# Delta rule: packed 32-key products sent between the stores and the scatters of the inverted blocks

## The reference

```python
def step(S, inp):
    qt, kt, vt, gt, bt = inp
    S = S * gt[..., None]
    pred = jnp.einsum('bhk,bhkv->bhv', kt, S)
    delta = (vt - pred) * bt[..., None]
    S = S + kt[..., None] * delta[:, :, None, :]
    o = jnp.einsum('bhk,bhkv->bhv', qt, S)
    return (S, o)
...
_, o = jax.lax.scan(step, S0, (tfirst(q), tfirst(k), tfirst(vf), tfirst(g), tfirst(beta)))
```

## Time and profile before

| | |
|---|---|
| median of 3 executions | 1822.89 us (1809.54 to 1831.44) |
| profiled execution, its own time | 1815.07 us |
| its span | 1813.3 us |
| TensorE, matmuls | 1519.7 us busy, 84% |
| VectorE | 1239.9 us busy, 68% |
| ScalarE | 1025.5 us busy, 57% |
| granted TensorE clock over the span | 0.881 |

### The profile page before, as it was taken

The page is one execution under the profiler, slowest core; times in us unless marked ns, Lnnn a source line. Parts: engine busy times, 40 slices in busy tenths (PEclk is TensorE's granted clock), DMA queues, the critical chain, the costliest instruction groups (busy, mean ns, idle before and its releaser), DMA issues. The chain is left out here.

```text
span 1813.3 us, 41435 instructions
## 1 busy us (share of the span) xinstructions
PE 1519.7 (84%) x14936; PEld 1014.4 (56%) x14936; DVE 1239.9 (68%) x3815; ACT 1025.5 (57%) x2716; POOL 41.2 (2%) x49
## 2 busy tenths in 40 slices
PE   6877889788797678888988888889888988878678
PEld 3534555564454245656666666666666666667435
DVE  5759989856723578777778867877866877864131
ACT  5417878876311556676666756667656656643210
POOL 0000000000000000000000000000000000000000
PEclk9888899889998689899889978989978988968599
DMA  3032000000101211111111111111210211110010
GB/s 149 25 74 69 10 10 4 2 1 1 73 0 27 68 18 44 49 46 27 51 42 31 57 50 17 55 53 22 55 48 16 60 48 18 46 24 14 1 49 23
DMA packets 118312, 67.18 MB, mean 37 GB/s; under 512 B 93648, under 2 KB 107216, under 8 KB 116960
## 3 DMA queue, kind: packets, MB, share of 16 engines
q1 hardware_dynamic: 118112, 64.54, 12.9%
HBM read 51.36 MB, written 6.98 MB: 32 GB/s over the span
## 5 line engine op out<-in xcount | busy, mean ns | idle before, releaser
L1576 DVE SCALAR_TENSOR_TENSOR arena<-arena 128x1024 f32<-128x1024 f32 x144 | 184.6, 1282 | 32.4 <-ACT arena L1151 31.0
L819 PE MATMUL bank<-xt,arena 128*128 128x512 f32 x384 | 195.3, 642 | 5.4 <-ACT arena L1143 4.0
L1654 DVE TENSOR_TENSOR arena<-arena 128x512 f32<-128x512 f32 x224 | 156.2, 697 | 14.6 <-PE bank L872 13.1
L669 PE MATMUL bank<-xt,arena 128*128 128x512 f32 x320 | 143.3, 604 | 3.8 <-DVE arena L1394 3.8
L819 PEld LDWEIGHTS bank<-xt,arena 128*128 128x128 f32 x384 | 72.7, 206 | 72.4 <-issue 70.9
L669 PEld LDWEIGHTS bank<-xt,arena 128*128 128x128 f32 x320 | 60.7, 194 | 87.2 <-issue 87.2
L688 PE MATMUL bank<-arena 128*128 128x256 f32 (+2 forms) x384 | 100.2, 409 | 6.2 <-DVE arena L1394 5.3
L1084 ACT ACTIVATE arena<-arena 128x128 f32<-128x128 f32 x256 | 99.1, 389 | 9.4 <-DVE arena L1504 9.4
L902 PE MATMUL bank<-arena 64*64 64x64 f32 x1024 | 50.4, 258 | 58.0 <-issue 55.2
L872 PEld LDWEIGHTS bank<-arena 128*32 128x32 f32 x5120 | 62.4, 120 | 65.4 <-issue 51.8
L1697 DVE SCALAR_TENSOR_TENSOR arena<-arena,bank 128x128 f32<-128x128 f32 x112 | 38.7, 345 | 87.0 <-PE bank L968 84.9
(11 more groups left out here) (170 smaller groups left out, 3516.3 us busy)
## 6 DMA issues: line engine op xcount, KB each, us to landing
arena<-d_w SPq DMA_DIRECT2D x16, 519.0 KB, 6.4
arena<-beta_scratch SPq DMA_DIRECT2D x16, 512.0 KB, 5.5
arena<-zero_scratch SPq DMA_DIRECT2D x14, 512.0 KB, 4.6
arena<-arena SPq DMA_DIRECT2D x64, 64.0 KB, 2.6
arena<-zero_scratch SPq DMA_DIRECT2D x15, 256.0 KB, 2.9
arena<-w_scratch SPq DMA_DIRECT2D x2, 1376.0 KB, 6.1
arena<-f_idx SPq DMA_DIRECT2D x2, 1072.0 KB, 11.9
w_scratch<-arena SPq DMA_DIRECT2D x2, 1072.0 KB, 4.0
```

The lines of the kernel that those rows point to most:

```text
L669: last = pe.matmul(bank[2 * w + n % 2][0:rows, :], (WU if f < 2 else WU1R)[:, w, k, m * P:m * P + rows], XT[:, k, hf * HALF:(hf + 1) * HAL ...
L819: last = pe.matmul(bank[b][:], DW[:, par, c:c + P], XT[:, k, rhs], start=(k == 0), stop=(k == KC - 1))
L1576: dve.scalar_tensor_tensor(out=CT[:, x], in0=RAW[:, x, 3 - j:3 - j + S], scalar=DW[:, par, tap:tap + 1], in1=CT[:, x], op0=ALU.mult, op1=A ...
L1654: dve.tensor_tensor(kq, kq, left, ALU.mult)
```

## The change

The four strip DMAs of a head, with the two waits ahead of them, move from a function of their own, called between `blocks` and `inverse`, into `inverse`: behind the two stores of the inverted blocks and ahead of the wait for the stores' landing. The number of DMAs, their sizes and their semaphores stay. Lines of the changed kernel behind the spot have other numbers: the stores are L545 and L546, the strips L552, the scatters L558 and L559.

```diff
--- before.py
+++ after.py
@@ -536,14 +536,6 @@
                     wait(sp, base_step, BASE_STEPS * m)
                     sp.dma_start(BL, blk_in.rearrange("b (j i) -> b j i", j=BLK)).then_inc(blocks_in, 16)
 
-                def strips(m, par):
-
-                    sp.wait_ge(strips_ready, 2 * m + 2)
-                    wait(sp, full[6], read(6, m - 2, "predict", NT - 1))
-                    for k in range(P // STRIP):
-                        ks = slice(STRIP * k, STRIP * (k + 1))
-                        sp.dma_start(MB[ks, par, :, :, ks], MBC[ks, par]).then_inc(strips_put, 16)
-
                 def inverse(m, par):
 
                     sp.wait_ge(base_step, BASE_STEPS * (m + 1))
@@ -552,6 +544,12 @@
                     wait(sp, y_put, 16 * NB * m)
                     sp.dma_start(blk_y.rearrange("b (c i) -> b c i", c=BLK), ZI).then_inc(inverse_out, 16)
                     sp.dma_start(blk_x.rearrange("b (i c) -> b i c", i=BLK), ZT).then_inc(inverse_out, 16)
+
+                    sp.wait_ge(strips_ready, 2 * m + 2)
+                    wait(sp, full[6], read(6, m - 2, "predict", NT - 1))
+                    for k in range(P // STRIP):
+                        ks = slice(STRIP * k, STRIP * (k + 1))
+                        sp.dma_start(MB[ks, par, :, :, ks], MBC[ks, par]).then_inc(strips_put, 16)
                     sp.wait_ge(inverse_out, 32 * (m + 1))
                     wait(sp, x_zero, 16 * m)
                     wait(sp, y_zero, 16 * (m - 1))
@@ -578,7 +576,6 @@
                     if m + 2 < H:
                         head(m + 2, m % 2)
                     blocks(m, m % 2)
-                    strips(m, m % 2)
                     inverse(m, m % 2)
                     if m + 2 < H:
                         gate_weights(m + 2, m % 2)
```

## The result

The changed kernel takes 1750.66 us, the median of 4 executions (1749.14 to 1755.34), against 1816.22 us of the kernel before on the same chip (1803.75 to 1831.44): a ratio of 0.9665 with a 95% interval of 0.9597 to 0.9734. Run again beside the later experiments it took 1752.17 us, a ratio of 0.9703 (0.9679 to 0.9727) to 1807.5 us. The prediction was 1749 us. The profiled execution after took 1755.34 us, the one before 1815.07. Ratios and their intervals are taken without the executions that a lower granted clock made slow, medians with them, so a ratio is not exactly the quotient of the medians beside it.

The account below looks back on a forecast made before the run. TensorE was taken to stand, with VectorE, for SyncE's DMA queue ahead of each head's first `left`. 1815.07 - 39.5 (chain) - 34 (clock) = 1741.6 us against the profiled execution, 1749 against the median; range 1730 to 1793 us.

Parts of the forecast that it names:

- What bounds the kernel: Ahead of each head's first `left`, TensorE (57.9 us in all) and VectorE (84.9 us) stand still for SyncE's queue.
- The stores go first: In SyncE's queue, stores issue inside the wait for level 4, so the first scatter goes 2.65 us earlier, 2.0 in head 0.
- How much of 2.65 us counts: At the first `left`, the earlier scatter counts only where TensorE pauses that long: 39.5 us over sixteen heads.
- TensorE's clock: Behind the first `left`, shorter pauses remove 87 us of low clock time, at 0.39 us each: 34 us.
- if low time moves into the levels: Sign of being wrong: low clock time turns up at the matmuls of the levels; no size given.
- the rival in which the clock gives nothing: In the delta rule, falls of the clock only move to the levels' small matmuls; 39.5 us remain, 1783 us; chance 0.25.
- The sum: Whole kernel: 1815.07 - 39.5 - 34 = 1741.6 us against the profiled execution, 1749 us against the median; chance 0.52.
- Chain alone: Whole kernel: the DMA chain shortens by 39.5 us and the clock gives nothing, 1783 us (1768 to 1795); chance 0.25.
- Nothing comes through: In SyncE's queue, transfers and not their issue hold the scatters; time stays within 1%, at 1823 us; chance 0.07.

Follow-up runs that it names:

- experiment 3: Changed kernel with each strip sent twice, the second time into columns that nothing reads: 1815.39 us, 0.9997 of the kernel before.
- experiment 4: Kernel before the change, with ten matmuls that nobody reads ahead of each head's first `left`: 1792.58 us, 0.9867 of the kernel before.
- experiment 10: Changed kernel with four matmuls that nobody reads ahead of level 0 of the second group: 1734.80 us, 0.9597 of the kernel before.
- experiment 1: Changed kernel with two of the four strips moved back ahead of the stores: 1778.99 us, 0.9801 of the kernel before.
- experiment 6: Changed kernel with the strips issued by GpSimd in place of SyncE: 1716.31 us, 0.9452 of the kernel before.
- experiment 5: Changed kernel with five matmuls that nobody reads ahead of the first `left` of even heads: 1751.97 us, 0.9653 of the kernel before.
- experiment 2: Changed kernel with the wait for the stores' landing put ahead of the strips: 1754.48 us, 0.9668 of the kernel before.

## Why the prediction came out

**What bounds the kernel: right.** TensorE and VectorE stood still for SyncE's queue ahead of the first `left`. With less queue both waits fell (from the 57.9 and 84.9 us of the earlier trace rows to 20.3 and 39.2), and with the queue time put back (experiment 3) the time was that of before.

**"The stores go first": right.** They went into the wait ahead of the strips, their landing (2.1 us) was covered by the strips' issue (2.67 us), and nothing waited longer. The first scatter was to go 2.65 us earlier; in head 5 it went 5.47 - 2.78 = 2.69, over the 16 heads 48.7 us, a mean of 3.0. The rest over 2.65 are mostly single slow issues of strips and stores, up to 1.79 us, and in head 3 a landing of 3.2 us; all of these stood in the way of the first scatter before, and fewer do now. In head 0 the strips were pushed back as said; they end 0.05 us ahead of the first scatter.

**"How much of 2.65 us counts", 39.5 us: right.** TensorE's pauses fell by 57.9 - 20.3 = 37.6 us, and the sixteen parts from a head's first L533 to its first `left` by 531.8 - 494.0 = 37.8 us. The pauses are 0 to 0.17 us in the odd heads but head 1, 1.4 to 2.8 in the even ones and in head 1, and 4.9 in head 0; forecast were 0 to 0.2, 1.2 to 2.4, and about 4.

**"TensorE's clock", 34 us: right in kind, too large.** This is the term that was mis-sized. It says "I count the falls behind L902 as gone" and took 87 us of low time off; the profiles show 66. Two steps failed. Behind the first `left` 62 us went and not 87: head 4 kept 6.8 us with a pause of 1.41, under the 2.1 us that were taken to be harmless; head 14 kept 15 where 4 were counted, and heads 6 and 10 6.8 each. And low time elsewhere was taken to stay as it is: at the levels it grew by 26 us, in the part ahead of `left` it shrank by 25. These two cancel, so that 66 in all is close to 62 by luck. The prediction had the levels as a way of being wrong ("if low time moves into the levels") and as the rival in which the clock gives nothing; the truth lies between the sum and that rival. On the two profiles the stretches behind `left`, where the prediction looked for the 34 us, are 489.1 - 471.1 = **18.0 us** shorter.

Its price, 0.39 us, was also high. Over 30 executions of the kernel before, the time rises with the low time (twice one less the granted clock, times the span) by 0.325 us per us, with a correlation of 0.94; the ten executions of experiment 3 give 0.37. Both figures are correlations between executions of one kernel, and without the four and the three slowest executions they are 0.29 and 0.35. The page "TensorE: Matmul & The Clock Gate" of the Trainium skill (section "HAM oscillation — how this bites in real kernels") prices low time at one half; these runs put it below. Where an edit took low time away it brought less: 110 us of it 22 us in experiment 4, and 79 us of it 18 us in experiment 10, each with a fill that itself costs time. From the mean of 412 us before to 342 after, 70 us at 0.325 to 0.37 are 23 to 26 us.

**The sum.** The means of all executions, 1814.4 and 1751.4 us, differ by 63 us: 23 to 26 of clock and 37 to 40 of chain, against 34 and 39.5. That split rests on the price. On the profiles the delta rule, from head 0's first L533 to head 15's `left`, lost 55.9 us: 37.8 of chain and 18.0 behind `left`. Another 7.1 us were gained ahead of head 0's first L533, at 638.15 and then 631.08 us, where the two kernels are the same: up to 577 us the profiled execution before had 102 us of low time and the one after 75, which is not the change's doing. The forecast gain, from 1822.89 to 1749, was 74 us, the measured one 66 between medians. That 1749 still stands so near to 1750.66 is in part luck: the kernel before came out at 1816.22 with one execution more, and the two differences cancel. Against the profiled execution, for which the sum gave 1741.6 us, the kernel took 1755.34, 13.7 us more.

**The rivals.** "Chain alone" (1783) was 32 us off, and experiment 4 shows that the clock is a term by itself: its interval, 0.9808 to 0.9925, excludes no change, with the DMA chain left as it was. "Nothing comes through" fell with the result and with experiments 1, 3 and 6: the time follows the issues in SyncE's queue. The page "DMA: Bandwidth & Descriptors" of the Trainium skill (section "Issuing engines are not separate DMA queues") calls the time for starting a DMA usually small relative to the DMA itself. For four issues of 0.64 us beside a landing of 2.5 us, one behind the other, that does not hold here.

**What stays open.** The gain by the clock is known only as 18 us (the two profiles) to 26 us (the price above). Why the pause of 1.11 us at the levels gives a fall of 10.2 us in some heads, of 3.4 in others and none in head 7 was not found. Whether filling the 2.5 us pauses pays was not settled (experiment 5), nor whether waiting for the stores first costs anything (experiment 2).

## What to carry to other kernels

- A queue of DMA issues is an engine with a list. Put what is ready early into the waits that the queue has anyway, and between an issue and the wait for its landing put the other issues; the price of an issue is read from the queue's rows, and it counts only as far as an engine pauses for the chain.
- A pause on TensorE costs its length and the lower clock behind it. Price both from the trace, and then look where the clock falls next: a clock gain counted at one site is partly given back at another, so count the low time over the whole stage. A few matmuls that nobody reads, in the pause ahead of narrow work, got back 17 us in one place and 16 to 24 in another, though they lasted nearly twice as long as planned; read their length from a trace and keep it under the pause, which no run here tried.
- After the first gain read the same chain again: another queue for four of the issues and eight of the scatters first brought 38 us more (1750.66 to 1712.48).

## What the runs showed of the hardware

- GpSimd issued a DMA in 0.65 us and its transfer landed after 2.9 us, against 0.64 and 2.5 us of SyncE for the same four transfers. In this kernel it was a second queue with issues as short as the first one's and landings 0.4 us later.
- An issue of SyncE that takes 0.64 us now and then takes much longer, at most 1.79 us before and 1.41 after, at the same line and size; what lengthens it was not found.
- One and the same kernel spread from 1798 to 1844 us over ten executions (experiment 3), and the time goes with the granted clock: 0.37 us for each us of low time, with a correlation of 0.98. Over the kernel before it is 0.325 us, with 0.94.
- Ten matmuls of 128x256 in float32 took 4.48 us at the full clock (experiment 4), and four took 1.99 us in most heads (experiment 10).
